# A decoder layer on one core: the shift seeds of two key blocks in eight written by TensorE instead of ScalarE

## The chip, the cores and the metric

The kernel runs on one core of one Trainium2 chip. The metric is the device time of one execution in microseconds (us), as the median of several. The inputs are those of the reference: `x` is 4 x 1024 x 256, the context 4 x 154 x 256, all float32.

## The reference, cut to what matters

Three sub-layers follow one another, each with a residual sum and a layer norm: self-attention with 16 heads of 64, a compressing memory layer, and a top-1 routed feed-forward layer with 8 experts. The change touches only the attention (and two scratch buffers of the router):

```python
q = jnp.einsum('bnd,hde->bhne', query, Wq) * scale      # scale = 1/8
k = jnp.einsum('bmd,hde->bhme', query, Wk)
v = jnp.einsum('bmd,hde->bhme', query, Wv)
logits = jnp.einsum('bhne,bhme->bhnm', q, k)
attn = jax.nn.softmax(logits, axis=-1)
out = jnp.einsum('bhnm,bhme->bnhe', attn, v)
```

A softmax may subtract any shift per query before the exponential. The kernel subtracts the maximum of the query's row.

## The kernel before, in words

**Units and blocks.** The attention is cut into 64 units. A unit `u` is one pair of heads of one batch with 512 of its 1024 queries. Its keys are cut into 8 blocks of 128, `kt` = 0 to 7, and the blocks are counted through all units as `n = 8u + kt`, 512 in all. A block of scores is laid out keys by queries: 128 partitions, two heads side by side of 512 queries, in one of two PSUM tiles `score_ps[n % 2]`.

**What happens to a block.** ScalarE first writes the negated row maxima, spread over all partitions in `shift_all`, into the PSUM tile: this is the seed (`seed`, L1336). TensorE then adds three products to it (`score`, L1214): queries and keys are each held as a high and a low part in float32r, and the products are high by high, high by low and low by high. Each head needs only 64 rows of the array, so the two heads' matmuls of a product run side by side. Then ScalarE takes the exponential into `probs`, a ring of eight (`exp`, L1325). GpSimd adds the blocks of a unit for the softmax sum (`add`, L1082 and L1086). TensorE multiplies with `v` (`weigh`, L1230) and, once per unit, turns the summed block into row sums by a matmul with ones (`total`, L1241), which waits for GpSimd's last add of that unit. The first two blocks of all, n = 0 and 1, have no seed by ScalarE: there TensorE adds a fourth product, ones by `shift_rows`.

**The shifts.** The row maxima come from extra score matmuls, the passes (`row_pass`, L1190), of high parts alone, done one or two units ahead. VectorE reduces each (L1395). When a unit's eight passes are done, SyncE writes the maxima to DRAM (`move_shift`, L953) and reads them back spread over the partitions (`spread_shift`, L958).

**The order.** All engines walk one list written by hand, `STEPS`, with a line for each half of a unit (four lines, repeated for each pair of heads). An `exp` follows each `score`, a `seed` follows each `exp`; the seed after the exponential of block n is that of block n + 2, because it takes the same PSUM tile. In three of the four lines two scores stand together, then their two exponentials, and later their two seeds. Between them stand the passes, the products for the next q, k and v (`bite`, L1167 and L1174), and the steps of the layer's later stages for the batch before (L446 and others). Three more PSUM banks, `spare_ps`, are passed round among passes, bites, sums and the later stages. The feed-forward tail starts after the last unit, near 1550 us.

Of the kernel before, what the change touches and what calls it, by code (L numbers as in the profile page):

```python
# [5 lines left out]
F32 = mybir.dt.float32  # L6
F32R = mybir.dt.float32r
ACT = mybir.ActivationFunctionType
# [3 lines left out]
P = 128  # L12
# [22 lines left out]
class Route:  # L35
# [8 lines left out]
    def __init__(self, nc, ctx, x, bp, ctx_in, conv_w, conv_b, Wg, Wp, oT_dram, xe_dram, const):  # L44
# [72 lines left out]
        self.dropped_before = sb("dropped_before", [P, TB])  # L117
        self.number = sb("number", [P, TB, EX])
        self.inside = self.shifted_logits
        self.kept = sb("kept", [P, TB, EX])  # L120
        self.row = sb("row", [P, TB])

        self.cw = [self.o_in[:, :, :, :].rearrange("p a c n -> p (a c n)")
# [556 lines left out]
def build_attention(nc, x, Wq, Wk, Wv, oT_dram, xT_dram, shift_dram, const, route, probs, v, weights, block, signals):  # L680
# [23 lines left out]
    PLACES = ("early", "late")  # L704
    BLOCK = 32
    SHARED = UNITS - 2
    LAST_TILES = TILES * (B - 1)
    assert 2 * E == P and KT == 8 and SCALE == 0.125 and N == 2 * BANK
    ident, ident_zeroed, ident_ready, one_rows = const
# [112 lines left out]
    with ExitStack() as ctx:  # L822
# [20 lines left out]
        max_of = sb("max_of", [P, 2, 2, JT, 2])  # L843
        neg_max = sb("neg_max", [P, BLOCK], F32R)
        neg_rows = sb("neg_rows", [P, BLOCK], F32R)
        shift_all = sb("shift_all", [P, 2, 2, BANK])
        shift_rows = route.o_hi[:, :, :].rearrange("p c n -> p (c n)")[:, 0:BANK]

        score_ps = [ctx.enter_context(nc.psum_tensor(f"score_ps{i}", [P, 2, BANK], F32)) for i in range(2)]
# [50 lines left out]
        o_done = sem("o_done")  # L900
        o_stored = [sem(f"o_stored{i}") for i in range(2)]

        def spare(step):

            return [spare_ps[bank] for bank in SPARE[step]]
# [16 lines left out]
        def _(sp):  # L922
# [31 lines left out]

            def spread_shift(u):
                sp.wait_ge(shift_out, 64 * (u + 1))
                wait(sp, seeded, KT * (u - 1) - 2)
                sp.dma_start(shift_all[:, u % 2], shift_dram[u % 2].rearrange("(a h) n -> a h n", a=1)  # L958
                             .broadcast_to([P, 2, BANK])).then_inc(shift_in[u % 2], 16)

            def store_o(u):
# [32 lines left out]
            load_w(1)  # L994
            load_wv(1)
            load_w(2)
            sp.wait_ge(rows_set, 2)
            move_first_shift()
            move_shift(0)
            spread_shift(0)  # L1000
# [51 lines left out]
        @block.gpsimd  # L1052
        def _(pool):
            def split_w(p):
                pool.wait_ge(w_loaded, 16 * 2 * KC * (p + 1))
                if p > 1:
                    pool.wait_ge(bite_ready, NUMBER["q", p - 2, 1] + 1)
                    pool.wait_ge(bite_ready, NUMBER["k", p - 2, 1] + 1)
                pool.tensor_copy(w_hi[:, p % 2], w_raw[:, :]).then_inc(w_split_hi, 1)
                pool.wait_ge(w_split_hi, p + 1)  # L1060
                pool.tensor_tensor(w_lo[:, p % 2], w_raw[:, :], w_hi[:, p % 2].bitcast(F32), ALU.subtract  # L1061
                                   ).then_inc(w_split, 1)

            def split_wv(t):
                pool.wait_ge(wv_loaded, 16 * KC * (t + 1))
                if t > 0:
                    pool.wait_ge(bite_ready, NUMBER["v", t - 1, 3] + 1)
                pool.tensor_copy(wv_hi[:, :, :], wv_raw[:, :, :]).then_inc(wv_split_hi, 1)
                pool.wait_ge(wv_split_hi, t + 1)
                pool.tensor_tensor(wv_lo[:, :, :], wv_raw[:, :, :], wv_hi[:, :, :].bitcast(F32), ALU.subtract  # L1070
                                   ).then_inc(wv_split, 1)

            def add(u, kt):

                n = KT * u + kt
                done = (KT - 1) * u + kt - 1
                heads = slice(0, 1 if u >= SHARED else 2)
                out = prob_sum[:, u % 2, heads]
                pool.wait_ge(probs_ready, n + 1)
                if kt == 1:  # L1080
                    wait(pool, sum_ready, u - 1)
                    pool.tensor_tensor(out, probs[:, (n - 1) % RING, heads], probs[:, n % RING, heads], ALU.add  # L1082
                                       ).then_inc(prob_added, 1)
                else:
                    pool.wait_ge(prob_added, done)
                    pool.tensor_tensor(out, out, probs[:, n % RING, heads], ALU.add).then_inc(prob_added, 1)  # L1086

            pool.memset(ident[:, :], 0.0).then_inc(ident_zeroed, 1)
            pool.wait_ge(ident_zeroed, 1)
            pool.affine_select(out=ident[:, :], in_=ident[:, :], compare_op=ALU.not_equal, fill=1.0,  # L1090
                               base=0, pattern=[[-1, P]], channel_multiplier=1).then_inc(ident_ready, 1)
            split_w(0)
            split_wv(0)
            split_w(1)
            pool.memset(neg_max[:, :].bitcast(F32), 0.0).then_inc(max_zeroed, 1)
            pool.memset(prob_sum[:, 0, 0, 0:P], 1.0).then_inc(rows_zeroed, 1)
            pool.memset(sums[:, :], 0.0).then_inc(rows_zeroed, 1)
            pool.wait_ge(rows_zeroed, 2)
            pool.tensor_copy(one_rows[:, :], prob_sum[:, 0, 0, 0:P]).then_inc(rows_set, 1)
            pool.tensor_copy(shift_rows, sums[:, :]).then_inc(rows_set, 1)  # L1100
            pool.wait_ge(rows_set, 2)
            for h in range(HALVES):
                u, second = divmod(h, 2)
                g, quarter = divmod(h, 4)
                if quarter == 0 and g % 2 == 0 and g // 2 + 1 < PAIRS // 2:
                    split_wv(g // 2 + 1)
                if quarter == 1 and g + 2 < PAIRS:
                    split_w(g + 2)
                for place in range(2):
                    for kt in range(KH * second + 2 * place, KH * second + 2 * place + 2):  # L1110
                        if kt > 0:
                            add(u, kt)
                    for name, *at in route_steps(h)[place]:
                        if name == "wp":
                            route.wp_low(pool, *at)
                        if name == "split":
                            route.split_low(pool, *at)
                        if name == "consts":
                            route.set_consts(pool)
                        if name == "bias":  # L1120
                            route.bias(pool, *at)
                        if name == "ids":
                            route.number_tokens(pool, *at)
                        if name == "moved":
                            b, i = at
                            for t in route.SUM_ORDER[2 * i:2 * i + 2]:
                                route.add_moved(pool, b, t, route.sum_done)
                        if name == "send":
                            route.send(pool, *at, route.sent)
                if HALVES - 10 <= h <= HALVES - 9:  # L1130
                    route.bias(pool, B - 1, h - HALVES + 10)

        @block.tensor
        def _(pe):
# [58 lines left out]
            def score(u, kt):  # L1193

                n = KT * u + kt
                par = u // 2 % 2
                keys = slice(kt * P, (kt + 1) * P)
                tokens = slice(u % 2 * BANK, (u % 2 + 1) * BANK)
                if kt == 0:
                    pe.wait_ge(bite_lo_done, lows_to(max(NUMBER["q", u // 2, u % 2], NUMBER["k", u // 2, 1])))  # L1200
                products = [(k_hi[:, par, keys], q_hi[:, par, tokens]), (k_hi[:, par, keys], q_lo[:, par, tokens]),
                            (k_lo[:, par, keys], q_hi[:, par, tokens])]
                if n < 2:
                    pe.wait_ge(first_shift, 64)
                    pe.wait_ge(xT_low_done, STAGED)
                    pe.wait_ge(bite_hi_done, EARLY)
                    pe.wait_ge(rows_set, 2)
                    products.append((one_rows[:, :], shift_rows))
                else:
                    pe.wait_ge(seeded, n - 1)  # L1210
                for i, (a, b) in enumerate(products):
                    for hd in range(2):
                        rows = slice(hd * E, (hd + 1) * E)
                        last = pe.matmul(score_ps[n % 2][:, hd, :], a[rows], b[rows], start=(n < 2 and i == 0),  # L1214
                                         stop=(i == len(products) - 1), skip_group_check=n > 1)
                last.then_inc(score_ready, 1)
# [84 lines left out]
        def _(act):  # L1301
# [25 lines left out]
            def seed(u, kt):  # L1327

                n = KT * u + kt + 2
                u, kt = divmod(n, KT)  # L1330
                if u == UNITS:
                    return
                if kt == 0 or n == 2:
                    act.wait_ge(shift_in[u % 2], 16 * (u // 2 + 1))
                act.wait_ge(probs_ready, n - 1)
                act.activation(score_ps[n % 2][:, :, :], shift_all[:, u % 2], ACT.Copy).then_inc(seeded, 1)  # L1336

            def raise_x(n):
                b, i = divmod(n, T_PAIRS)
# [825 lines left out]
```

## Time and profile before

| What | Value |
|---|---|
| Time, three runs | 1797.97 us median, 1796.36 to 1801.69 |
| Profiled execution, its own time | 1796.57 us |
| Its span, first to last instruction | 1794.8 us |
| Mean granted TensorE clock | 0.995 |
| TensorE matmuls (PE) busy | 1728.4 us, 96% |
| TensorE weight loads (PEld) busy | 1062.3 us, 59% |
| ScalarE (ACT) busy | 1299.0 us, 72% |
| GpSimd (POOL) busy | 1383.5 us, 77% |
| VectorE (DVE) busy | 1149.7 us, 64% |

A row of a group view gives line, engine, operation, what it writes and reads, the count, the busy time and the mean ns of one, and then the engine's idle time just before. A row of the timeline gives the start in us, the duration, and in brackets the idle time before it and what ended it. Matmul durations overlap, so how close the starts stand says more than the durations do.

### The profile page before, as it was taken

The numbers are of one execution on the slowest core, as the hardware profiler recorded it, in microseconds if no ns is written. First come the engines' busy times: TensorE is split into PE (matmuls) and PEld (weight loads), VectorE is DVE, ScalarE is ACT, GpSimd is POOL, SyncE is SP. The second block draws the span as 40 slices with busy tenths as digits, with TensorE's granted clock in tenths as the row PEclk, the third lists the DMA queues.
The fourth block names the chain that finished last, engine by engine and source line by source line (L and its number), as shares of the span: only waits on it lengthen the run. The fifth ranks groups of instructions, "written<-read, shape, count | busy, mean of one in ns | idle before, by whom it ended". The sixth has DMA issues, their size and how long they took to land.

```text
span 1794.8 us, 29382 instructions
## 1 busy us (share of the span) xinstructions
PE 1728.4 (96%) x10380; PEld 1062.3 (59%) x10380; DVE 1149.7 (64%) x2122; ACT 1299.0 (72%) x1602; POOL 1383.5 (77%) x735
## 2 busy tenths in 40 slices
PE   6999999999999999999999999999999998999998
PEld 5555555555665555556655555556655554598887
DVE  5666666666556657766556667755566678675565
ACT  3687777777668777777667877776687877665674
POOL 2688888889887978899788878899888777641664
PEclk9999999999999999999999999999999999999999
DMA  4421111113312111133222111232222111633441
GB/s 135 144 61 42 48 42 48 42 48 99 131 52 79 48 42 48 45 107 128 70 69 67 42 48 42 57 100 77 65 70 67 54 39 56 198 109 127 144 142 36
DMA packets 142933, 137.72 MB, mean 77 GB/s; under 512 B 60741, under 2 KB 121285, under 8 KB 141765
## 3 DMA queue, kind: packets, MB, share of 16 engines
q1 hardware_dynamic: 139716, 127.38, 23.7%
q0 software_dynamic: 3072, 8.46, 1.3%
q8 instruction: 86, 1.41, 0.3%
q14 instruction: 59, 0.48, 0.1%
HBM read 102.70 MB, written 29.69 MB: 74 GB/s over the span
## 4 chain that ended last, share of the span: by engine, by line
PE 59%; POOL 24%; issue 7%; ACT 3%; DMA 3%; DVE 3%; SPq 1%; POOLq 0%; DVEq 0%; ACTq 0%
POOL prob_sum L1086 17%; PE av_ps L1230 15%; PE score_ps L1214 12%; PE spare_ps L1174 6%; PE spare_ps L1190 6%; PE y_ps L1816 4%; PE h_ps L1787 4%; PE spare_ps L1167 3%; PE spare_ps L1241 3%; PE spare_ps L446 2%; ACT probs L1325 2%; DMA x<-x 1%; DVE max_of L1395 1%; POOL prob_sum L1082 1%; POOL w_lo L1061 1%
## 5 line engine op out<-in xcount | busy, mean ns | idle before, releaser
L1086 POOL TENSOR_TENSOR prob_sum<-prob_sum,probs 128x1024 f32<-128x1024 f32 (+1 forms) x384 | 903.2, 2352 | 157.4 <-ACT probs L1325 122.7
L1395 DVE TENSOR_REDUCE max_of<-spare_ps 128x1 f32<-128x512 f32 x1024 | 655.2, 681 | 280.2 <-PE spare_ps L1190 275.9
L1325 ACT ACTIVATE probs<-score_ps 128x1024 f32<-128x1024 f32 x512 | 502.6, 1022 | 284.6 <-PE score_ps L1214 279.7
L1336 ACT ACTIVATE score_ps<-shift_all 128x1024 f32<-128x1024 f32 x510 | 511.3, 1030 | 1.1
L1230 PE MATMUL av_ps<-probs,v 128*64 128x512 f32 x2048 | 489.5, 603 | 0.5 <-ACT probs L1325 0.5
L1230 PEld LDWEIGHTS av_ps<-probs,v 128*64 128x64 f32 x2048 | 130.3, 136 | 242.7 <-issue 199.2
L1190 PE MATMUL spare_ps<-k_hi,q_hi 64*128 64x512 f32 x1024 | 231.3, 446 | 20.6 <-DVE max_of L1395 17.8
L1190 PEld LDWEIGHTS spare_ps<-k_hi,q_hi 64*128 64x128 f32 x1024 | 98.2, 184 | 224.1 <-issue 179.6
L1214 PE MATMUL score_ps<-q_hi,k_hi 64*128 64x512 f32 x1024 | 211.9, 409 | 3.7 <-ACT score_ps L1336 3.7
L1214 PE MATMUL score_ps<-q_hi,k_lo 64*128 64x512 f32 x1024 | 203.4, 392 | 0.0
L1214 PE MATMUL score_ps<-q_lo,k_hi 64*128 64x512 f32 x1024 | 202.6, 391 | 0.0
L1082 POOL TENSOR_TENSOR prob_sum<-probs 128x1024 f32<-128x1024 f32 (+1 forms) x64 | 150.6, 2354 | 59.3 <-ACT probs L1325 58.7
L1174 PE MATMUL spare_ps<-xT_kept,w_hi 128*128 128x512 f32 x496 | 155.4, 405 | 1.5 <-issue 1.0
L1214 PEld LDWEIGHTS score_ps<-q_hi,k_hi 64*128 64x128 f32 x1024 | 96.7, 185 | 42.9 <-ACT score_ps L1336 25.6
L1214 PEld LDWEIGHTS score_ps<-q_hi,k_lo 64*128 64x128 f32 x1024 | 97.1, 185 | 22.5
L1214 PEld LDWEIGHTS score_ps<-q_lo,k_hi 64*128 64x128 f32 x1024 | 97.2, 186 | 16.9
L1174 PEld LDWEIGHTS spare_ps<-xT_kept,w_hi 128*128 128x128 f32 x496 | 86.7, 190 | 30.6 <-issue 17.3
L1382 DVE SCALAR_TENSOR_TENSOR q_lo<-spare_ps,q_hi 128x512 fp32r<-128x512 f32 x62 | 42.9, 691 | 91.4 <-ACT q_hi L1312 90.0
L1167 PE MATMUL spare_ps<-wv_hi,xT_kept 128*128 128x256 f32 x488 | 91.1, 289 | 0.1
L1241 PE MATMUL spare_ps<-prob_sum,ones 128*64 128x512 f32 x256 | 68.8, 616 | 19.3 <-POOL prob_sum L1086 18.2
L1167 PEld LDWEIGHTS spare_ps<-wv_hi,xT_kept 128*128 128x128 f32 x488 | 72.9, 190 | 13.4 <-issue 11.1
L1174 PE MATMUL spare_ps<-xT_kept,w_lo 128*128 128x512 f32 x248 | 77.8, 395 | 0.0
(278 smaller groups left out, 2272.8 us busy)
## 6 DMA issues: line engine op xcount, KB each, us to landing
shift_all<-shifts SPq DMA_DIRECT2D x64, 512.0 KB, 4.0
o_transposed<-sums SPq DMA_DIRECT2D x64, 256.0 KB, 4.0
v<-in_L_ffn_W_dram SPq DMA_DIRECT2D x16, 1024.0 KB, 5.9
o_in<-o_transposed SPq DMA_DIRECT2D x28, 512.0 KB, 4.3
w_raw<-in_L_attn_Wq_dram SPq DMA_DIRECT2D x64, 64.0 KB, 3.0
w_raw<-in_L_attn_Wk_dram SPq DMA_DIRECT2D x64, 64.0 KB, 2.8
wv_raw<-in_L_attn_Wv_dram SPq DMA_DIRECT2D x32, 128.0 KB, 3.9
shifts<-neg_rows SPq DMA_DIRECT2D x256, 1.0 KB
```

Of the source, the lines that this page charges most:

```text
L1082: pool.tensor_tensor(out, probs[:, (n - 1) % RING, heads], probs[:, n % RING, heads], ALU.add).then_inc(prob_added, 1)
L1086: pool.tensor_tensor(out, out, probs[:, n % RING, heads], ALU.add).then_inc(prob_added, 1)
L1167: last = pe.matmul(bank[:, m * 4 * E:(m + 1) * 4 * E], xT[batch][:, half, kc, rows], w[:, kc, :], start=(i == 0 and kc == 0), stop=(i == 2 ...
L1174: last = pe.matmul(bank[:, :], w[:, of % 2, "qk".index(kind), kc, :], xT[batch][:, half, kc, cols], start=(i == 0 and kc == 0), stop=(i == ...
L1190: pe.matmul(bank[:, :], q_hi[rows, par, tokens], k_hi[rows, par, keys], start=True, stop=True).then_inc(pass_ready, 1)
L1214: last = pe.matmul(score_ps[n % 2][:, hd, :], a[rows], b[rows], start=(n < 2 and i == 0), stop=(i == len(products) - 1), skip_group_check= ...
L1230: last = pe.matmul(av_ps[hd * E:(hd + 1) * E, :], v[:, quad % 2, kt, 2 * first_head + hd, :], probs[:, n % RING, hd, :], start=(kt == 0), ...
L1241: last = pe.matmul(bank[hd * E:(hd + 1) * E, :], ones[:, 0:E], prob_sum[:, u % 2, hd, :], start=True, stop=True)
L1325: act.activation(probs[:, n % RING], score_ps[n % 2][:, :, :], ACT.Exp).then_inc(probs_ready, 1)
L1336: act.activation(score_ps[n % 2][:, :, :], shift_all[:, u % 2], ACT.Copy).then_inc(seeded, 1)
L1395: dve.tensor_reduce(max_of[:, u % 2, kh, j, hd:hd + 1], bank[:, :], AX.X, ALU.max).then_inc(pass_read, 1)
L1787: last = pe.matmul(h_bank(p, c)[:, rows], w[x][:, k, c * P:(c + 1) * P], xeT[y][:, k, rows], start=(i == 0 and k == 0), stop=(i == 2 and k ...
```

## The change

Blocks with `kt` 2 and 6 (n > 2) get no seed from ScalarE. For these TensorE issues a fourth product first, `shares` by `shift_all`, with start=True: `shares` is 1/64 everywhere, and the 64 rows that a head's matmul covers all hold the same shift, so their sum is the shift. `shift_all` is now typed float32r. In those blocks TensorE waits for the exponential of block n - 2, where it waited for the seed. GpSimd makes `shares` at the start. SyncE's transfer of new shifts waits for the seeds and now also for the scores of the unit whose shifts it writes over. Two router buffers share one place. That makes 2 blocks in each of 64 units less n = 2, 127 blocks.

```diff
-        self.kept = sb("kept", [P, TB, EX])
+        self.kept = self.logits
...
+    MULTIPLIED = (2, 6)
...
-        shift_all = sb("shift_all", [P, 2, 2, BANK])
+        shift_all = sb("shift_all", [P, 2, 2, BANK], F32R)
+        shares = sb("shares", [P, P], F32R)
...
+        def multiplied(n):
+
+            return n > 2 and n % KT in MULTIPLIED
+
+        def seeds_to(n):
+
+            return sum(not multiplied(m) for m in range(2, n + 1))
...
             def spread_shift(u):
                 sp.wait_ge(shift_out, 64 * (u + 1))
-                wait(sp, seeded, KT * (u - 1) - 2)
-                sp.dma_start(shift_all[:, u % 2], shift_dram[u % 2].rearrange("(a h) n -> a h n", a=1)
+                wait(sp, seeded, seeds_to(KT * (u - 1) - 1))
+                wait(sp, score_ready, KT * (u - 1))
+                sp.dma_start(shift_all[:, u % 2].bitcast(F32), shift_dram[u % 2].rearrange("(a h) n -> a h n", a=1)
                              .broadcast_to([P, 2, BANK])).then_inc(shift_in[u % 2], 16)
...
-            pool.wait_ge(rows_zeroed, 2)
+            pool.memset(prob_sum[:, 0, 1, 0:P], 1.0 / E).then_inc(rows_zeroed, 1)
+            pool.wait_ge(rows_zeroed, 3)
+            pool.tensor_copy(shares[:, :], prob_sum[:, 0, 1, 0:P]).then_inc(rows_set, 1)
...
                     products.append((one_rows[:, :], shift_rows))
+                elif multiplied(n):
+                    if kt == 0:
+                        pe.wait_ge(shift_in[u % 2], 16 * (u // 2 + 1))
+                    pe.wait_ge(probs_ready, n - 1)
                 else:
-                    pe.wait_ge(seeded, n - 1)
+                    pe.wait_ge(seeded, seeds_to(n))
+                if n > 1 and multiplied(n):
+                    for hd in range(2):
+                        rows = slice(hd * E, (hd + 1) * E)
+                        pe.matmul(score_ps[n % 2][:, hd, :], shares[rows, :], shift_all[rows, u % 2, hd, :],
+                                  start=True, stop=False, skip_group_check=True)
...
-                if u == UNITS:
+                if u == UNITS or multiplied(n):
                     return
-                if kt == 0 or n == 2:
+                if kt == min(set(range(KT)) - set(MULTIPLIED)) or n == 2:
                     act.wait_ge(shift_in[u % 2], 16 * (u // 2 + 1))
                 act.wait_ge(probs_ready, n - 1)
-                act.activation(score_ps[n % 2][:, :, :], shift_all[:, u % 2], ACT.Copy).then_inc(seeded, 1)
+                act.activation(score_ps[n % 2][:, :, :], shift_all[:, u % 2].bitcast(F32), ACT.Copy).then_inc(seeded, 1)
```

## Rows read from the trace of the kernel before

**Rows 1.** The page: busy time of each engine, then the chain's shares by engine.

```profile
PE 1728.4 (96%) x10380; PEld 1062.3 (59%) x10380; DVE 1149.7 (64%) x2122; ACT 1299.0 (72%) x1602; POOL 1383.5 (77%) x735
...
PE 59%; POOL 24%; issue 7%; ACT 3%; DMA 3%; DVE 3%; SPq 1%; POOLq 0%; DVEq 0%; ACTq 0%
```

**Rows 2.** The page's costliest groups: ScalarE's exponentials and its seeds.

```profile
L1325 ACT ACTIVATE probs<-score_ps 128x1024 f32<-128x1024 f32 x512 | 502.6, 1022 | 284.6 <-PE score_ps L1214 279.7
L1336 ACT ACTIVATE score_ps<-shift_all 128x1024 f32<-128x1024 f32 x510 | 511.3, 1030 | 1.1
```

**Rows 3.** Timeline, TensorE, 37 to 40 us: two blocks of four products each.

```profile
37.43 0.40 PE L1214 MATMUL score_ps<-q_hi,k_hi 64*128 64x512 f32 x2
...
38.12 0.41 PE L1214 MATMUL score_ps<-o_hi,ones 64*128 64x512 f32 x2
38.35 0.41 PE L1214 MATMUL score_ps<-q_hi,k_hi 64*128 64x512 f32 x2
...
39.27 0.49 PE L1190 MATMUL spare_ps<-k_hi,q_hi 64*128 64x512 f32 x2
```

**Rows 4.** Timeline, TensorE, unit 22, blocks 0 and 1, from pass to pass.

```profile
550.81 0.50 PE L1190 MATMUL spare_ps<-k_hi,q_hi 64*128 64x512 f32 x2
551.15 0.39 PE L1214 MATMUL score_ps<-q_hi,k_hi 64*128 64x512 f32 x2
...
552.52 0.40 PE L1190 MATMUL spare_ps<-k_hi,q_hi 64*128 64x512 f32 x2
```

**Rows 5.** Timeline, ScalarE and TensorE, unit 22, around blocks 2 and 3.

```profile
552.05 1.94 ACT L1325 ACTIVATE probs<-score_ps 128x1024 f32<-128x1024 f32 x2 [1.25 <-PE score_ps L1214]
...
553.88 1.98 ACT L1336 ACTIVATE score_ps<-shift_all 128x1024 f32<-128x1024 f32 x2
...
554.72 0.49 PE L1190 MATMUL spare_ps<-k_hi,q_hi 64*128 64x512 f32 x2
...
555.53 0.40 PE L1214 MATMUL score_ps<-q_hi,k_lo 64*128 64x512 f32 x2
555.91 0.19 PEld L1214 LDWEIGHTS score_ps<-q_hi,k_hi 64*128 64x128 f32 x2 [0.41 <-ACT score_ps L1336]
...
556.71 0.40 PE L1190 MATMUL spare_ps<-k_hi,q_hi 64*128 64x512 f32 x2
```

**Rows 6.** Waits, whole span: us in total, times, longest us.

```profile
POOL prob_sum L1086 <- ACT probs L1325: 122.7, 96, 7.1
...
PEld score_ps L1214 <- ACT score_ps L1336: 25.6, 54, 2.5
...
PE spare_ps L1241 <- POOL prob_sum L1086: 18.2, 17, 2.1
...
PE score_ps L1214 <- ACT score_ps L1336: 3.7, 6, 2.0
```

**Rows 7.** Waits, 300 to 1500 us.

```profile
PEld score_ps L1214 <- ACT score_ps L1336: 13.4, 36, 0.9
```

**Rows 8.** Waits, 1495 to 1560 us.

```profile
PEld score_ps L1214 <- ACT score_ps L1336: 9.1, 10, 2.5
```

**Rows 9.** Chain of waits, 500 to 560 us: start, us, what.

```profile
518.01 2.38 POOL prob_sum L1086
...
525.56 2.39 POOL prob_sum L1086
...
527.99 1.08 PE spare_ps L1241 x4
```

**Rows 10.** Chain of waits, 1510 to 1545 us.

```profile
1533.76 0.93 ACT score_ps L1336
...
1541.70 1.02 ACT probs L1325
```

**Rows 11.** Timeline, GpSimd, first 40 us.

```profile
22.96 0.29 POOL L1099 CAST ones<-prob_sum 128x128 fp32r<-128x128 f32 x1
...
35.56 0.61 POOL L1068 CAST wv_hi<-wv_raw 128x512 fp32r<-128x512 f32 x1 [11.75 <-PE spare_ps L1167]
```

More of the change, by code:

```diff
@@ L996, in _ @@
             load_w(2)
-            sp.wait_ge(rows_set, 2)
+            sp.wait_ge(rows_set, 3)
             move_first_shift()
@@ L1097, in _ @@
             pool.memset(sums[:, :], 0.0).then_inc(rows_zeroed, 1)
-            pool.wait_ge(rows_zeroed, 2)
+            pool.memset(prob_sum[:, 0, 1, 0:P], 1.0 / E).then_inc(rows_zeroed, 1)
+            pool.wait_ge(rows_zeroed, 3)
+            pool.tensor_copy(shares[:, :], prob_sum[:, 0, 1, 0:P]).then_inc(rows_set, 1)
             pool.tensor_copy(one_rows[:, :], prob_sum[:, 0, 0, 0:P]).then_inc(rows_set, 1)
             pool.tensor_copy(shift_rows, sums[:, :]).then_inc(rows_set, 1)
-            pool.wait_ge(rows_set, 2)
+            pool.wait_ge(rows_set, 3)
             for h in range(HALVES):
@@ L1206, in score @@
                     pe.wait_ge(bite_hi_done, EARLY)
-                    pe.wait_ge(rows_set, 2)
+                    pe.wait_ge(rows_set, 3)
                     products.append((one_rows[:, :], shift_rows))
-                else:
-                    pe.wait_ge(seeded, n - 1)
+                elif multiplied(n):
+                    if kt == 0:
+                        pe.wait_ge(shift_in[u % 2], 16 * (u // 2 + 1))
+                    pe.wait_ge(probs_ready, n - 1)
+                else:
+                    pe.wait_ge(seeded, seeds_to(n))
[4 more added lines that the diff above has]
+                                  start=True, stop=False, skip_group_check=True)
                 for i, (a, b) in enumerate(products):
```

## The prediction, made before the changed kernel was run

> **What bounds the kernel now.** I read the page's busy times first, then the chain of waits, then who waits for whom, and last the timeline of single units. The page shows TensorE's matmuls busy for 96% of the span and ScalarE for 72%; the chain runs over TensorE for 59% of the span, over GpSimd for 24% and over ScalarE for only 3% [rows 1]. The costliest groups and the waits say the same from the other side: ScalarE stood idle for 279.7 us before exponentials because a score was not ready [rows 2], while the score matmuls stood idle for a seed for 3.7 us [rows 6]. So ScalarE mostly waits for TensorE, and hardly the other way. Busy time alone would not prove that TensorE is full, since its durations overlap; the starts do. In unit 22, from the pass at 550.81 to the pass at 552.52, two blocks of scores take 1.71 us with no gap [rows 4].
>
> GpSimd bounds some of the units. In unit 20 its adds stand end to end from 518.01 and the sum's matmul starts the moment the last of them ends, at 527.99 [rows 9]. TensorE waits so for GpSimd 17 times, 18.2 us in all [rows 6].
>
> The change gives ScalarE, which has room, less to do, and gives TensorE, which has little, more. The question is how much of the addition falls into time that TensorE now spends waiting.
>
> **What is added on TensorE.** Each of 127 blocks gets one product more, of the shape 64x128 by 64x512, two heads at once. The kernel before has exactly this in its first two blocks: from 37.43 to 38.35 a block with four products takes 0.92 us, the next, from 38.35 to the pass at 39.27, again 0.92, so 0.23 us for a product [rows 3]. Both run at full clock in a stretch without waits. 127 x 0.23 = **+29.2 us**. The bounds: the product might cost as much as the step from a pass to the first score, 0.34 us (550.81 to 551.15) [rows 4], because it opens the block and comes behind another weight load; that is 127 x 0.34 = 43.2 us. It can't cost less than nothing. I take 0.23, since it is the same kind of instruction in the same place, and since the first product of a block already pays for the step from the pass: the new one takes over that place and pushes the others back by one slot.
>
> **What goes on ScalarE.** 127 copies of 1.03 us, 131 us [rows 2]. ScalarE is on the chain for 3%, so this is worth only what was waiting for these copies. There are three places.
>
> (a) *Waits for a seed in the bulk.* In unit 22 the exponentials of blocks 0 and 1 start at 552.05 and end at 553.99, and the seeds of blocks 2 and 3 follow from 553.88 for 1.98 us, until 555.86. Block 2 starts just as its seed is there, block 3 has to wait for its own: its weights load at 555.91, after 0.41 us of idle [rows 5]. From pass to pass this pair took 1.99 us (554.72 to 556.71), against 1.71 without the wait [rows 4, 5], so 0.28 us is really lost, less than the 0.41 idle of the weight loads, which otherwise load ahead. After the change block 2 needs no seed and block 3's seed starts one copy (1.03 us) sooner, so the wait goes altogether; what is late next there is nothing of ScalarE's, but TensorE's own sequence with 0.23 more. From 300 to 1500 us there are 36 such waits [rows 7], in the whole span 54 plus 6 [rows 6], of which ten or so at the end are another case (b). Some 45 x 0.28 = 12.6 us; a few of them stand before other blocks than 3 and 7 or are shorter, so 10 us. A quarter of the chain runs over GpSimd, where TensorE's gain is not the end's: 0.75 x 10 = **-7.5 us**. Bounds: from 3.7 us, the idle that the matmuls themselves show, to 29.3 us, both wait rows in full [rows 6].
>
> (b) *The last units.* From 1510 us on few other products are left between the scores, and exponential, seed and score follow one another on the chain. Of the last unit's seeds two go: the one at 1533.76 for 0.93 us, which is block 2's, and block 6's, which now stands in front of the exponential at 1541.70 [rows 10]. Each gives some 1 us, against products of 0.23 that are counted above: **-2 us**. All the waits of this stretch together are 9.1 us [rows 8]; most stand before blocks 4 and 5, whose seeds stay.
>
> (c) *ScalarE earlier elsewhere.* The exponential of the first block of a pair starts when its score is ready, not when ScalarE is free (idle of 1.25 us before the one at 552.05 [rows 5]). So the exponentials don't come earlier, nor does what GpSimd and `weigh` do behind them: nothing. Without this cover, if exponentials did start earlier, it would be a gain: the rival below.
>
> **What GpSimd's stretches hide.** Where TensorE waits at the sum for GpSimd, work that TensorE got since GpSimd last waited for an exponential costs nothing. Two blocks of a unit carry 2 x 0.23 = 0.46 us. Of the 17 waits, 1.07 us long on average [rows 6], some 14 have GpSimd busy without a break for about a unit before, as in unit 20 [rows 9]; 14 x 0.46 = 6.4, **-6.5 us**. Bounds: 0, if each sum is tied to an exponential behind a fourth product, to 64 x 0.46, all of it. I take what the 17 waits allow. In the many other units GpSimd itself waits for the exponentials (122.7 us in 96 waits [rows 6]), which TensorE's scores start: there the addition shifts everything.
>
> **The small edits.** At the start GpSimd clears one more 128x128 piece and converts it, like the cast of 0.29 us at 22.96; behind it GpSimd waits for TensorE for 11.75 us at 35.56 [rows 11], and TensorE's and SyncE's waits on `rows_set` come at 37 us: nothing (0.5 us if the cover were gone). SyncE's new wait for `score_ready` concerns scores of the unit before the running one, which are done when the maxima come; behind it in SyncE's queue stand stores of o and loads of weights, which are not held up. The wait of the fourth product, for the exponential of block n - 2, comes one copy earlier than the seed that it replaces. The shared buffer adds no instruction. Together nothing.
>
> **The sum.** 29.2 - 7.5 - 2 - 6.5 = +13.2 us. The profiled execution took 1796.57 us, 1.77 more than its span, so 1809.8 for the changed kernel, and as the median of the runs lies 1.40 us above the profiled one, 1811 us.
>
> The Trainium skill (Perfetto Trace Analysis, Identifying the Most-Contended Engine) says that matmul busy time is a bad measure of how full TensorE is, that the weight loads' busy share should be used, and that the engine of highest occupancy is to be relieved first. By the page of the profile that would be 59% for TensorE, behind GpSimd's 77% and ScalarE's 72% [rows 1], and the change would move work to the less loaded engine. The starts of the matmuls in [rows 4] speak against it here; it is the reading on which the third rival rests.
>
> **The rivals.**
>
> *Nothing is hidden.* The full 29.2 us comes through, because the seed's waits are absorbed elsewhere and each sum hangs on an exponential that a fourth product delays: 1797.97 + 29 = 1827 us. For it: 59% of the chain on TensorE, GpSimd's 96 waits for exponentials. Against it: the 0.28 us of [rows 4, 5], which can be seen.
>
> *A draw.* The waits for seeds come back in full, 25.6 + 3.7 = 29.3 us against 29.2 [rows 6]: 1798 us. For it: the wait rows taken at their word. Against it: the weight load's idle of 0.41 us was 0.28 of lost time, and part of these waits are before blocks whose own seed remains.
>
> *Faster: ScalarE's relief lets GpSimd start earlier.* The mechanism is the exponential's start. If the 131 us of copies taken away let exponentials start sooner, GpSimd's adds and with them the sums come sooner, and the 18.2 us that matmuls wait at the sum go, on top of the draw: 1798 - 18 = 1780 us. It decides from the point where exponentials now start later than 0.1 us or so after their score because a seed is in front of them. For it: GpSimd's 24% of the chain, and the seeds keep ScalarE itself for 511.3 us with next to no idle time in front (1.1 us [rows 2]). Against it: in a pair the second exponential stands behind the first and not behind a seed, as at 552.05 [rows 5].
>
> **How the numbers follow.** The forecast (part hidden) 0.63, nothing hidden 0.18, the draw 0.11, the faster rival 0.08. What a measurement of this kernel can tell from no change is about 0.3%, 5.4 us: 1792.6 to 1803.4. Faster 0.08, same 0.12, slower 0.80. The range goes from 1802, where (a) is worth 16 us and not 7.5, to 1826, nearly nothing hidden.
>
> **What would show it.** Right: seeds x383, score matmuls of `shares` by `shift_all` x254, blocks of four products 0.23 us longer than those of three; no weight load of block 3 waiting for a seed, pass to pass of blocks 2 and 3 about 1.95 us; TensorE's wait for GpSimd at the sum down from 18.2 to about 12 us; ScalarE's idle time before exponentials up by 130 us or more. Wrong: if the fourth product costs 0.3 us or more, or if the exponentials move nearer to their scores.

## The result and the profile after

The changed kernel takes 1808.93 us (median, 1807.73 to 1811.32) against 1798.38 us for the kernel before: a ratio of 1.0062, 95% interval 1.0047 to 1.0077, so slower by 8 to 14 us. The forecast was 1811 us. Its profiled execution has a span of 1807.2 us, 12.4 more than the 1794.8 of before, at the same mean clock of 0.995.

The page of the changed kernel, the rows that answer to [rows 1]:

```profile
PE 1744.4 (97%) x10634; PEld 1089.5 (60%) x10634; DVE 1149.5 (64%) x2122; ACT 1189.0 (66%) x1475; POOL 1383.0 (77%) x737
...
PE 63%; POOL 23%; issue 5%; DVE 3%; DMA 3%; ACT 3%; SPq 0%; POOLq 0%; DVEq 0%; ACTq 0%
```

ScalarE lost 110 us of busy time, and its share of the chain, 3%, is what it was. TensorE has 254 matmuls more, and its share of the chain rose from 59% to 63%. The costliest groups show the same for exponentials and seeds, as in [rows 2]:

```profile
L1347 ACT ACTIVATE probs<-score_ps 128x1024 f32<-128x1024 f32 x512 | 498.6, 1022 | 386.2 <-PE score_ps L1236 378.3
...
L1358 ACT ACTIVATE score_ps<-shift_all 128x1024 f32<-128x1024 f32 x383 | 388.6, 1029 | 3.0
```

ScalarE's freed time turned into waiting: its idle time before exponentials grew by 101.6 us (284.6 to 386.2). An exponential still takes 1022 ns.

One exponential in sixteen does run sooner. The fourth line of `STEPS`, unlike the others, has for blocks 4 and 5 an exponential, a seed and an exponential, so in every second unit ScalarE wrote the seed of block 6 between the two exponentials. Unit 21 before, ScalarE and then GpSimd:

```profile
538.62 1.02 ACT L1325 ACTIVATE probs<-score_ps 128x1024 f32<-128x1024 f32 x1 [1.48 <-PE score_ps L1214]
539.68 1.03 ACT L1336 ACTIVATE score_ps<-shift_all 128x1024 f32<-128x1024 f32 x1
540.65 1.01 ACT L1325 ACTIVATE probs<-score_ps 128x1024 f32<-128x1024 f32 x1
...
539.73 4.92 POOL L1086 TENSOR_TENSOR prob_sum<-prob_sum,probs 128x1024 f32<-128x1024 f32 x2 [2.03 <-ACT probs L1325]
```

and in the changed kernel:

```profile
542.25 1.94 ACT L1347 ACTIVATE probs<-score_ps 128x1024 f32<-128x1024 f32 x2 [1.48 <-PE score_ps L1236]
...
543.36 4.91 POOL L1097 TENSOR_TENSOR prob_sum<-prob_sum,probs 128x1024 f32<-128x1024 f32 x2 [2.26 <-ACT probs L1347]
```

The exponential of block 5 started 2.03 us after that of block 4 and now starts 0.92 us after it, in all 32 odd units. Nothing came of it: GpSimd's add of block 4 takes 2.46 us (4.92 for two) and starts 1.11 us after its exponential in both kernels, and the add of block 5 comes right behind it. In all 30 odd units below unit 60 block 5's exponential had been done for 0.6 us or more before its add could start, in the kernel before already.

The timeline of TensorE in unit 22 of the changed kernel, blocks 2 and 3, which is the place of [rows 5]:

```profile
558.57 0.51 PE L1203 MATMUL spare_ps<-k_hi,q_hi 64*128 64x512 f32 x2
558.91 0.39 PE L1231 MATMUL score_ps<-shift_all,shares 64*128 64x512 f32 x2
559.14 0.39 PE L1236 MATMUL score_ps<-q_hi,k_hi 64*128 64x512 f32 x2
...
559.84 0.39 PE L1236 MATMUL score_ps<-q_hi,k_hi 64*128 64x512 f32 x2
...
560.53 0.39 PE L1203 MATMUL spare_ps<-k_hi,q_hi 64*128 64x512 f32 x2
```

The new product takes 0.23 us (558.91 to 559.14). Block 3 starts at 559.84 right behind block 2, without a wait for its seed. From pass to pass it is 1.96 us, where it was 1.99 with one product less [rows 5]. Here the addition cost nothing at all. The waits, whole span and then 300 to 1500 us, against [rows 6, 7]:

```profile
PEld score_ps L1236 <- ACT score_ps L1358: 6.8, 15, 2.5
...
PE spare_ps L1263 <- POOL prob_sum L1097: 14.0, 20, 1.6
```

```profile
PEld score_ps L1236 <- ACT score_ps L1358: 2.3, 10, 0.9
```

The waits for seeds fell from 25.6 to 6.8 us, in the bulk from 13.4 to 2.3, those for GpSimd at the sum from 18.2 to 14.0.

Where the time came from is read best from one mark per unit, the sum's matmul: how far it has moved tells what has piled up by then. The first sum, that of unit 19, that of unit 60 and the last one, in the kernel before:

```profile
73.65 1.03 PE L1241 MATMUL spare_ps<-prob_sum,ones 128*64 128x512 f32 x4
...
500.70 1.08 PE L1241 MATMUL spare_ps<-prob_sum,ones 128*64 128x512 f32 x4
...
1491.22 1.03 PE L1241 MATMUL spare_ps<-prob_sum,ones 128*64 128x512 f32 x4
...
1549.06 1.03 PE L1241 MATMUL spare_ps<-prob_sum,ones 128*64 128x512 f32 x4
```

and in the changed one:

```profile
72.52 1.03 PE L1263 MATMUL spare_ps<-prob_sum,ones 128*64 128x512 f32 x4
...
504.21 1.08 PE L1263 MATMUL spare_ps<-prob_sum,ones 128*64 128x512 f32 x4
...
1502.99 1.03 PE L1263 MATMUL spare_ps<-prob_sum,ones 128*64 128x512 f32 x4
...
1558.78 1.03 PE L1263 MATMUL spare_ps<-prob_sum,ones 128*64 128x512 f32 x4
```

The changed kernel is 1.1 us ahead at the first sum, 3.5 behind at unit 19, 11.8 behind at unit 60, and 9.7 at the last. So 12.9 us pile up in the bulk, about 0.21 a unit out of the 0.46 that its two products take, 2 us come back in the last units, and the other 2.6 us arise in the tail behind the last sum, which the change does not touch. The pile does not grow evenly. In unit 20, GpSimd's unbroken run of [rows 9] stands in the changed kernel too, and ends in the same way; the chain of waits there, 500 to 565 us:

```profile
521.40 2.38 POOL prob_sum L1097
...
528.96 2.41 POOL prob_sum L1097
...
531.41 1.08 PE spare_ps L1263 x4
```

Its sum is 3.42 us later than before (527.99 to 531.41), where the sum before it was 3.51 later: in this unit nothing was added.

### The profile page after: what moved, and what is told of

Same layout as the page of the kernel before. It is cut to its first block, busy times and chain, and to the rows that moved or that the text cites. A ratio compares the mean times of both kernels' runs of the same rounds, so it can differ in the third digit from the quotient of the medians.

```text
span 1807.2 us, 29765 instructions
## 1 busy us (share of the span) xinstructions
PE 1744.4 (97%) x10634; PEld 1089.5 (60%) x10634; DVE 1149.5 (64%) x2122; ACT 1189.0 (66%) x1475; POOL 1383.0 (77%) x737
## 4 chain that ended last, share of the span: by engine, by line
PE 63%; POOL 23%; issue 5%; DVE 3%; DMA 3%; ACT 3%; SPq 0%; POOLq 0%; DVEq 0%; ACTq 0%
POOL prob_sum L1097 17%; PE av_ps L1252 16%; PE score_ps L1236 12%; PE spare_ps L1203 6%; PE spare_ps L1187 6%; PE y_ps L1838 5%; PE h_ps L1809 4%; PE spare_ps L1180 3%; PE spare_ps L1263 3%; PE spare_ps L446 2%; ACT probs L1347 1%; DVE max_of L1417 1%; POOL w_lo L1072 1%; PE score_ps L1231 1%; DMA x<-x 1%
## 5 line engine op out<-in xcount | busy, mean ns | idle before, releaser
L1347 ACT ACTIVATE probs<-score_ps 128x1024 f32<-128x1024 f32 x512 | 498.6, 1022 | 386.2 <-PE score_ps L1236 378.3
L1358 ACT ACTIVATE score_ps<-shift_all 128x1024 f32<-128x1024 f32 x383 | 388.6, 1029 | 3.0
L1236 PE MATMUL score_ps<-q_hi,k_hi 64*128 64x512 f32 x1024 | 206.1, 399 | 2.9 <-ACT score_ps L1358 2.9
L1180 PEld LDWEIGHTS spare_ps<-wv_hi,xT_kept 128*128 128x128 f32 x488 | 72.8, 190 | 13.4 <-issue 11.1
```

Of the source, the lines that this page charges most:

```text
L1180: last = pe.matmul(bank[:, m * 4 * E:(m + 1) * 4 * E], xT[batch][:, half, kc, rows], w[:, kc, :], start=(i == 0 and kc == 0), stop=(i == 2 ...
L1347: act.activation(probs[:, n % RING], score_ps[n % 2][:, :, :], ACT.Exp).then_inc(probs_ready, 1)
```

## The experiments

Three sets: the parts of the change, each alone, with GpSimd's work as it is; other places for the product; and the parts once more with GpSimd's work cut down. Each was timed in five rounds against the kernel before. In the kernels without the change's ScalarE part, `MULTIPLIED` is empty.

**The small edits alone.**

```diff
-    MULTIPLIED = (2, 6)
+    MULTIPLIED = ()
```

> The changed kernel with no block multiplied: the list of such blocks is empty, so all 510 seeds are ScalarE's again; the start's extra cast, the shared router buffer and SyncE's extra wait stay. Every theory: the small edits cost nothing, so the time of before, 1798 us within 0.3%. If it is more than 3 us above, part of the 10.6 us belongs to them.

Measured: 1798.06 us, ratio 0.9998 (0.9989 to 1.0007). The small edits are free. Its profiled execution is 2.7 us longer than that of before nevertheless: at the last sum it stands 3.0 us ahead, and in the tail it falls 5.7 behind. The work of the two tails is the same, and what differs is the clock granted to TensorE. The windows 1590 to 1615 us, of the kernel before and then of this one (before the DMA share and GB/s comes the clock):

```profile
1590.00:1615.00 25.00, 23.33 (x164) 22.03 (x163) 20.26 (x68) 15.44 (x31) 5.46 (x5) 0.93 0.17 56
```

```profile
1590.00:1615.00 25.00, 23.32 (x132) 22.43 (x130) 15.96 (x49) 12.54 (x25) 1.79 (x2) 0.73 0.14 48
```

A clock of 0.73 in place of 0.93 is 5 us more of full-speed time lost in 25. The changed kernel's tail, 2.6 us longer than before, has a mean clock of 0.98 where before has 0.99. The lead at the start goes the same way: the first sum stands at 73.7 us at a clock of 0.95 (before), at 71.2 at 0.98 (the next experiment) and at 74.9 at 0.91 (the one after it); the changed kernel's 1.1 us, at 0.95, are not explained by it. From sum to sum, up to unit 60, the small edits alone agree with before within 0.2 us, but for 0.3 us in unit 20 and 1.1 us in unit 36, whose cause is open.

**The seeds of blocks 2 and 6 away, nothing in their place.**

```diff
-                if n > 1 and multiplied(n):
-                    for hd in range(2):
-                        rows = slice(hd * E, (hd + 1) * E)
-                        pe.matmul(score_ps[n % 2][:, hd, :], shares[rows, :], shift_all[rows, u % 2, hd, :],
-                                  start=True, stop=False, skip_group_check=True)
...
-                                         start=(n < 2 and i == 0),
+                                         start=(i == 0 and (n < 2 or multiplied(n))),
```

> Blocks 2 and 6 get neither a seed nor the fourth product (their shift is left out of the output's softmax). Theory A (relief is only what waited for seeds): the waits of the bulk give back 7.5 us and the last units 2 to 3, so -10 us, 1788. Rival B (ScalarE's relief lets exponentials and GpSimd start earlier): -25 us or more. Rival C (TensorE's waits for seeds are all absorbed elsewhere): 1798, no change. After minus this run is then the price of the product with its cover: A 21 to 23 us, of the 29.2 gross.

Measured: 1792.97 us, ratio 0.9973 (0.9960 to 0.9986), 5 us faster by the ratio (3 to 7): half of what A said, and far from B. The wait for seeds went as it did in the changed kernel; so where is the time? In its waits over the whole span:

```profile
PEld spare_ps L1258 <- POOL prob_sum L1097: 45.3, 32, 2.8
PE spare_ps L1258 <- POOL prob_sum L1097: 21.9, 24, 1.9
...
PEld score_ps L1231 <- ACT score_ps L1353: 6.6, 12, 2.5
```

The matmuls' wait for GpSimd at the sum is longer than before, 21.9 us against 18.2 [rows 6]. The timeline shows one unit of it. The kernel before, unit 12 and its sum:

```profile
324.25 9.94 POOL L1086 TENSOR_TENSOR prob_sum<-prob_sum,probs 128x1024 f32<-128x1024 f32 x4
...
334.24 0.20 PEld L1241 LDWEIGHTS spare_ps<-prob_sum,ones 128*64 128x64 f32 x4 [0.96 <-POOL prob_sum L1086]
```

The kernel without these seeds:

```profile
320.99 9.95 POOL L1097 TENSOR_TENSOR prob_sum<-prob_sum,probs 128x1024 f32<-128x1024 f32 x4
...
330.99 0.20 PEld L1258 LDWEIGHTS spare_ps<-prob_sum,ones 128*64 128x64 f32 x4 [1.24 <-POOL prob_sum L1097]
```

The last four adds of the unit run without a break, and the sum follows them. TensorE arrives 0.28 us sooner, the wait that it was spared at block 3, and stands 0.28 us longer (1.24 against 0.96). The saved wait was paid back at the sum. The marks say so for the whole loop: from the first sum to that of unit 60 this kernel gains 2.6 us, where the small edits alone gain 1.8.

**The product on blocks 2 and 6, the seeds kept.** `shares` is 0, so ScalarE's seed stays as it is.

```diff
+    EXTRA = (2, 6)
...
-            pool.memset(prob_sum[:, 0, 1, 0:P], 1.0 / E).then_inc(rows_zeroed, 1)
+            pool.memset(prob_sum[:, 0, 1, 0:P], 0.0).then_inc(rows_zeroed, 1)
...
-                if n > 1 and multiplied(n):
+                if n > 2 and kt in EXTRA:
...
-                                  start=True, stop=False, skip_group_check=True)
+                                  start=False, stop=False, skip_group_check=True)
```

> Blocks 2 and 6 keep ScalarE's seed and get a fourth product on top, with shares of 0, so it adds nothing to the value. Theory A (it is the removal of the seeds that gives 9.5 us back): without it the addition is 29.2 less what GpSimd's stretches hide, 6.5: +22.7, 1821 us. Rival D (the product itself fills the wait: while TensorE works on the fourth product of block 2, the seed of block 3 gets done): the wait is gone here too, so about the time of the changed kernel plus the 1 to 2 us of the last units, 1810 us.

Measured: 1813.72 us, ratio 1.0076 (1.0062 to 1.0090), +13.7 us and not +22.7. ScalarE makes all 510 seeds and still the price is within 3 us of the changed kernel's. Its timeline in unit 22 shows why:

```profile
561.36 0.50 PE L1204 MATMUL spare_ps<-k_hi,q_hi 64*128 64x512 f32 x2
...
562.54 0.19 PEld L1237 LDWEIGHTS score_ps<-q_hi,k_hi 64*128 64x128 f32 x2 [0.19 <-ACT score_ps L1359]
...
563.35 0.40 PE L1204 MATMUL spare_ps<-k_hi,q_hi 64*128 64x512 f32 x2
```

Pass to pass is 1.99 us, as without the product [rows 5]. The weight load of block 3 still waits for the seed, 0.19 us and not 0.41: the product of block 2 fills the time.

**The product on blocks 0 and 4, the seeds kept.** The same edit with `EXTRA = (0, 4)`.

> The same product of shares 0, on blocks 0 and 4 (128 less 0 for n=0: 127 blocks), which have no wait for a seed behind them in the bulk. Theory A, the GpSimd term: 29.2 less 6.5 hidden behind GpSimd's stretches, +22.7, 1821 us. Rival (nothing is hidden by GpSimd): +29, 1827. Rival D for the seeds says the same as A here; if e3 and e4 agree, D is wrong, if e3 is 8 us or more below e4, D is right.

Measured: 1819.13 us, ratio 1.0109 (1.0094 to 1.0123), +20 us. That is 6 us above the same product on blocks 2 and 6, in the direction of D but short of the 8 that were to decide; with light adds below it is 12. Between the first sum and that of unit 60 the two lie 4.4 us apart. And it is 9 to 10 us short of 29.2, more than the 6.5 that I had put down to GpSimd.

**The change on blocks 3 and 7.**

```diff
-    MULTIPLIED = (2, 6)
+    MULTIPLIED = (3, 7)
```

> Blocks 3 and 7 are multiplied in place of 2 and 6: the same 29 us of products (128 of them), the same number of seeds gone. Theory D (what a product costs depends on whether it stands in front of an exponential that GpSimd waits for; blocks 2 and 6 do, 3 and 7 stand behind it, where GpSimd is busy until the sum in every other unit at least): cheaper than the 10.6 us of the changed kernel, +5 to +8, 1805. Theory A (hidden are two blocks per wait of TensorE for GpSimd, whichever they are, and block 3's wait for its seed goes either way): +11, 1809.

Measured: 1806.64 us, ratio 1.0045 (1.0029 to 1.0061), +8 us, against 8 to 14 for blocks 2 and 6. The direction is that of D, but the intervals overlap, so the times alone don't show it. The profiles point the same way: from the first sum to that of unit 60 this kernel falls back 7.2 us, the changed one 12.9. Of these 5.7 us some 1.4 stand at units 20 and 36, where the small edits alone jump too. The clearest place is the even units 6 to 16, in which GpSimd's last adds run without a break to a sum that TensorE waits for: there this kernel loses 0.1 us in all and the changed one 1.5, while in the odd units between them both lose 0.4 each.

**Only the last two units multiplied.**

```diff
-    MULTIPLIED = (2, 6)
+    MULTIPLIED = ()
...
-            return n > 2 and n % KT in MULTIPLIED
+            return n >= KT * (UNITS - 2)
```

> Only the 16 blocks of the last two units are multiplied, all of each unit, none before. There exponential, seed, score follow one another on the chain. If ScalarE's seeds are really on the path there, some 4 to 5 copies of 1.0 us leave it against products of 0.23, partly in waits: -3 us, 1795.5. If the exponentials alone bound it, 0 to +2.

Measured: 1798.99 us, ratio 1.0003 (0.9985 to 1.0022). No gain that can be measured. In the profile the last two units are 1.0 us shorter than before, but with the small edits alone they are 0.6 us shorter too. ScalarE's copies stand on the chain there in the kernel before [rows 10]; with the small edits alone the chain of 1505 to 1548 us shows them too. Here GpSimd stands in their place, with its adds and with `expert_rows`, the rows that it sends for the router:

```profile
1538.52 1.25 POOL expert_rows L435
1539.79 1.30 POOL prob_sum L1097
...
1541.26 1.55 POOL prob_sum L1097
...
1542.95 1.26 POOL expert_rows L435
```

**GpSimd's adds cut down, nothing multiplied.** This takes the limit away instead of arguing about it. From the third block of a unit on GpSimd adds 64 of the 512 queries of each head.

```diff
-                    pool.tensor_tensor(out, out, probs[:, n % RING, heads], ALU.add).then_inc(prob_added, 1)
+                    pool.tensor_tensor(out[:, :, 0:E], out[:, :, 0:E], probs[:, n % RING, heads, 0:E], ALU.add
+                                       ).then_inc(prob_added, 1)
```

> GpSimd's adds from the third block of a unit on take only 64 of 512 queries of each head (the softmax sums of the others are left short), so GpSimd no longer bounds any unit; no block is multiplied. The waits for GpSimd at the sum (18.2 us, and more at the weight loads) go: -20 us or so, 1778. It is the base for the next run.

Measured: 1772.53 us, ratio 0.9852 (0.9829 to 0.9875), 26 us faster. GpSimd is busy for 37% of the span, and TensorE waits for it at no sum. Something else has grown in its waits:

```profile
PEld score_ps L1237 <- ACT score_ps L1359: 35.3, 78, 2.1
```

35.3 us in 78 waits for seeds, where there were 25.6 in 54 [rows 6]. Block 3 waits for its seed in 60 units here and waited in 33 before. The sum of a unit stands among the first blocks of the next one; unit 12's sum waited, and block 3 of unit 13 then found its seed ready. Where TensorE is no longer late at the sum, it has to wait for the seed.

**Light adds, blocks 2 and 6 multiplied.** The change and the edit above.

> The same light adds with blocks 2 and 6 multiplied. What counts is the distance to the run before it. If GpSimd's stretches hide part of the products (A and D), without them the distance is the 29.2 us less only what the waits for seeds take in: 19 to 21 us. If they hide nothing, it is the 10.6 us of the two full kernels.

Measured: 1785.93 us, ratio 0.9931 (0.9913 to 0.9949). Against the base with light adds that is 0.9931 / 0.9852 = 1.0080, +14 us with some 5 either way. I had expected 19 to 21, and the interval takes in the 11 of the full kernels; so this distance settles nothing, because two things moved: GpSimd's cover went, and waits for seeds came in its place. The next three take these apart. The marks have less noise: from the first sum to that of unit 60 the distance is 11.5 us, where the full kernels have 12.9.

**Light adds, product on blocks 0 and 4, seeds kept.**

> Light adds on GpSimd, as in the base with light adds and no block multiplied (1772.5 us, ratio to before 0.985), ScalarE's seeds all kept, and the product of shares 0 on blocks 0 and 4. No wait for GpSimd and no wait for a seed lies behind these products. Theory E (a product costs 0.23 us whole wherever TensorE has no wait after it; GpSimd's stretches took the missing 9.6 us in the same experiment with full adds): 29 us above the base, 1801.5. If GpSimd's stretches were not what hid it: 19.6 above, 1792.

Measured: 1803.84 us, ratio 1.0023 (1.0012 to 1.0035), 31 us above the base, 26 to 35. This is the full price, 127 x 0.23 = 29.2, which the prediction had read from two blocks; by the marks it is 27.5 us for the 120 products of units 1 to 60, 0.23 for each. The same edit cost 20 us with full adds, 17.9 by the marks: GpSimd's stretches hid 8 to 10 us, the lower figure if the two jumps of units 20 and 36 are left out.

**Light adds, seeds of blocks 2 and 6 away, nothing in their place.**

> Light adds, blocks 2 and 6 without seed and without product. Theory E (with full adds the 0.28 us that block 3 no longer waits for its seed is given back at the sum, where TensorE then waits longer for GpSimd; without GpSimd in the way it is kept): about 64 x 0.27 = 17 us below the base, 1755.5, against 4.9 us in the same experiment with full adds. Rival (ScalarE's seeds simply hold up little): 5 us below the base, 1767.5.

Measured: 1759.20 us, ratio 0.9779 (0.9762 to 0.9796), 13 us below the base, 8 to 18. With full adds the same edit gave 5 us. The end of ScalarE's waits is worth something when GpSimd doesn't take it back. By the marks it is 13.0.

**Light adds, product on blocks 2 and 6, seeds kept.**

> Light adds, ScalarE's seeds all kept, the product of shares 0 on blocks 2 and 6. Theory D (the product of block 2 stands in the time in which block 3 would wait for its seed, so the wait is gone without any relief of ScalarE): the same as the kernel with light adds and both edits, 14 us above the base (ratio to before 0.993). Theory A (only the removal of the seeds gives that time back): the full price, 29 to 31 us above the base, as on blocks 0 and 4 (ratio 1.002).

Measured: 1790.37 us, ratio 0.9959 (0.9947 to 0.9972), 19 us above the base. On blocks 0 and 4 it was 31. So 12 us of the product fall into waits for seeds although ScalarE is relieved of nothing; relief adds another 5 (14 against 19, within the error of both). By the marks it is 27.5, 14.0 and 11.5 us: the product fills 13.5, relief adds 2.5. D is the larger part, A the smaller. That A has a part is seen in the waits: 74 of them are left here, with 18.2 us, because 0.23 us of product does not fill a wait of 0.28, or one of 0.41 at the weight loads.

**Sharing GpSimd's adds with VectorE.** An attempt to use the 26 us, on the kernel before.

```diff
-    SHARED = UNITS - 2
+    SHARED = UNITS - 20
```

> The kernel before, untouched in its seeds; VectorE takes over the second head's adds in the last 20 units in place of the last 2. If GpSimd's adds are the dearest thing in the way (26 us with light adds), the 18 units more, with GpSimd's add at half the size, gain up to 18/64 of that, -7 us, 1791; but VectorE gets seven adds of 0.7 us more in each unit, before it reads the passes that TensorE waits for, and that can cost as much: +5.

Measured: 1853.68 us, ratio 1.0300 (1.0273 to 1.0327), 54 us slower. TensorE's waits for VectorE before the passes went from 17.8 to 42.8 us, and GpSimd's own for exponentials from 122.7 to 261.2. VectorE's adds stand in front of its reading of the passes, in order, and hold TensorE up. That is not the whole of it, for the granted clock fell too. Over the shared units, from the sum of unit 43 to that of unit 60, it is 0.97 where before has 1.00, and in the tail, whose work is the same, 0.95 against 0.99; that tail alone is 10.7 us longer. How the 54 us divide between waits and clock was not tried. None of the versions tried beats the kernel before, apart from those that leave work out.

In one table, in us from the base of the same adds (1798 full, 1772.5 light), by the ratios, and behind them by the marks from the first sum to that of unit 60 of one profile each:

| Edit | Full adds | by marks | Light adds | by marks |
|---|---|---|---|---|
| Product on 0 and 4, seeds kept | +20 | +17.9 | +31 | +27.5 |
| Product on 2 and 6, seeds kept | +14 | +13.5 | +19 | +14.0 |
| Seeds of 2 and 6 away, no product | -5 | -2.6 | -13 | -13.0 |
| Both: the change | +11 | +12.9 | +14 | +11.5 |

The small edits alone are at 0 by the ratio and at -1.8 by the marks.

## Why the prediction was right, and where it was right for the wrong reason

*TensorE bounds the kernel, ScalarE has room.* Right. 122.7 us of seeds less on ScalarE (511.3 to 388.6) gave 5 us by themselves, 3 to 7.

*The product costs 0.23 us, 29.2 in all.* Right, in the timeline (558.91 to 559.14) and by the run with light adds (+31 us where nothing hides it).

*(a) The waits for seeds in the bulk give 7.5 us back.* The step whose mechanism was wrong in part. The wait went and the pair of blocks takes 1.96 us, as forecast (1.95). But I gave this to ScalarE's relief. The product alone, all seeds kept, does nearly the same, since it stands in the very time in which TensorE would wait. And relief alone gives its time back at the next sum in units like unit 12, where GpSimd sets the pace. The size was off too: between the product on blocks 0 and 4 and the changed kernel lie 5.0 us by the marks, not 7.5. Block 3 waited in 33 units, where the prediction had taken some 45 waits.

*(b) The last units give 2 us.* About right in size, but not by the figure that lies nearest. The changed kernel gains 2.1 us on before between the sum of unit 60 and the last; the small edits alone gain 1.4 there with every seed in place, and their clock is 0.97 where before has 0.94. Against the same products with the seeds kept, also at 0.97, it is 1.4 us. More of the same brought nothing.

*(c) No exponential comes sooner.* Wrong as a statement, right in what it is worth. The prediction looked at a pair that stands together, and in the odd units blocks 4 and 5 do not: block 5's exponential moved 1.1 us nearer to block 4's and to its own score. That is what the prediction had named as a sign of being wrong, and the condition of its faster rival. The rival fell all the same, because GpSimd was still busy with block 4's add whenever block 5's exponential came: the removal of the seeds with nothing in their place is the most that it could give, and that is 5 us, not 18 beyond the draw. That this term came out at nothing was luck in part.

*GpSimd's stretches hide 6.5 us.* Right in kind, a little too small: for the product on blocks 0 and 4 it is 8 to 10 us. The marks show where. In the 17 units in which the matmuls waited at the sum the product costs 7.5 us with light adds and with full ones nothing (-1.2, the two jumps among them). In the 13 in which only the weight loads waited, like unit 12, it costs 5.8 and 3.7; in the other 30 of units 1 to 60, 14.1 and 15.4, so what the 13 hide is for the larger part paid in the others. Two products for each waiting unit was the right rule, and all 17 units should have been counted, not 14.

*The sum.* Hidden are 29.2 less the 11 of the ratio, 18 us (15 to 21), against a forecast of 16. The total lies nearer than its terms deserve: the waits for seeds were put too high by 2.5 us and GpSimd's cover too low by 1.5 to 3, and these errors have opposite signs. Nor do covers add up when each is taken alone: by the marks GpSimd hides 8 to 10 us of a product, and the waits for seeds give back 16 us of the change's product when GpSimd is out of the way, but only 5 when it is not. Each unit has one delay to give, and product, relief and GpSimd compete for it.

*The signs.* Seeds x383 and 254 new matmuls: right. GpSimd's wait at the sum "down to about 12": 14.0. Block 3's wait gone and 1.96 us from pass to pass: right. ScalarE's idle time before exponentials up by 130 us: it was 101.6. Its idle time as a whole grew by 122.4 us, the 110.0 that its busy time fell and the 12.4 that the span grew; of the rest 17.9 stand before the copies of v (L1329: 19.5, where L1307 had 1.6). The 131 us of copies are 127 durations, and with their overlaps they were only 122.7 us of busy time. "Wrong if the exponentials move nearer to their scores": one in sixteen did, as told under (c).

The Trainium skill (Perfetto Trace Analysis, Identifying the Most-Contended Engine) judges TensorE's headroom by the weight loads' share and by the matmul work done against peak, not by matmul busy time. The weight loads' share alone, 59%, would have let work be moved to TensorE for little. The runs decide against that reading here: a product with no wait behind it cost its whole 0.23 us.

## What to carry to other kernels

Before moving work from an engine with room to the one that sets the pace, ask what the first engine's release is worth alone: here 5 us for 123 us of work. Look at every place in which the released engine's instructions stand, not at one. A wait that is removed counts only up to the next wait behind it; where another engine runs without a break up to a join, the saved time comes back as a longer wait at that join. And if an addition falls into a wait, it is free with or without the relief that came with it, so test the two halves apart before crediting one.

## What the runs showed of the hardware beyond expectation

Most of the spread of one and the same kernel goes with the clock granted to TensorE. The kernel before was timed 67 times beside the experiments. The eleven executions with a mean clock of 0.995 took 1793.7 to 1796.5 us, the seven with 0.989 or 0.990 took 1801.5 to 1806.2 us.

So the profiles of two kernels are best compared with the clock of the same stretch beside them. The tail of the same work took 245.8 us at 0.99 (before), 248.4 at 0.98 (the changed kernel), 251.5 at 0.97 (small edits alone) and 256.5 at 0.95 (adds shared with VectorE). The clock has two levels there, 2.4 and 1.2 GHz: in the profile of the small edits alone, matmuls of L1838 start 0.21 us apart at 1604 us and 0.12 us apart at 1609. In the middle of the loop the clock stands at 1.00 in before, in the changed kernel and in the small edits alone, and there neighbouring sums of the small edits alone and of before agree within 0.1 us in 57 of the 60 steps up to unit 60. It was these that carried the reading.
